# A merge of two instruction chains with its time slots halved, in an eight-core attention and gated-layer kernel

## The reference

```python
q  = apply_rope((x @ Wq + bq).reshape(B, T, 16, 64))
kv = ((x @ Wdown + bdown) @ Wup + bup).reshape(B, T, 16, 128)
k, v = split(kv); k = apply_rope(k)
att = softmax(einsum('bthd,btgd->bthg', q, k) / sqrt(64))   # heads against heads, per token
out = einsum('bthg,btgd->bthd', att, v).reshape(B, T, 1024) @ Wout + bout
x = layernorm(x + out)
x = layernorm(x + (silu(x @ wg.T) * (x @ wu.T)) @ wd.T)     # hidden 3072, integer weights / 127
```

## Time and profile before

| what | value |
|---|---|
| two timed runs | 3500.82 and 3587.18 us, median 3544.0 |
| the profiled execution's own time | 3500.25 us |
| its span on the slowest core | 3498.3 us |
| spans of the eight cores | 3476.4 to 3498.3 us |
| busy on that core: TensorE, VectorE, ScalarE, GpSimd | 2680.8, 1668.9, 803.4, 292.4 us |
| main part, tile 0 | 345 to 687 us from the span's start |
| tiles 1 to 7 | 687 to 3240 us |
| the last gated layer alone | 3240 us to the end |

### The profile page before, as it was taken

How to read it: one execution, slowest core, us unless ns; L and a number is a source line. 1 busy time by engine, 2 the same in 40 slices (tenths; PEclk the granted TensorE clock), 3 DMA queues, 4 the chain that set the end, 5 groups by cost and what they waited for, 6 DMA issues and landing times.

```text
span 3498.3 us, 41206 instructions; the slowest of 8 cores (3476.4 to 3498.3 us)
## 1 busy us (share of the span) xinstructions
PE 2680.8 (77%) x12416; PEld 1057.4 (30%) x12416; DVE 1668.9 (48%) x2454; ACT 803.4 (23%) x1361; POOL 292.4 (8%) x540
## 2 busy tenths in 40 slices
PE   0000686789888999799979998998889888988566
PEld 0000212233333333333333333333333333333222
DVE  2221355455546545474637454655565546554312
ACT  0000310142115130513042303330243124221101
POOL 0111000001100110011001100010001100110110
PEclk9999956599999999999999999999999999999778
DMA  6887200212332232323141223223322322231222
GB/s 192 244 243 206 56 1 25 42 48 62 97 73 82 61 86 77 92 63 89 61 112 52 73 82 100 64 61 94 89 77 61 100 64 82 64 97 55 93 78 82
DMA packets 108701, 303.92 MB, mean 87 GB/s; under 512 B 16192, under 2 KB 24768, under 8 KB 108496
## 3 DMA queue, kind: packets, MB, share of 16 engines
q1 hardware_dynamic: 61520, 169.14, 17.2%
q0 software_dynamic: 46976, 132.15, 13.0%
HBM read 269.77 MB, written 39.85 MB: 89 GB/s over the span
## 4 chain that ended last, share of the span: by engine, by line
PE 61%; DMA 11%; DVE 8%; issue 6%; ACT 4%; DVEq 0%; ACTq 0%; POOLq 0%; POOL 0%; SPq 0%
PE P L448 10%; PE P L762 9%; PE P L395 9%; PE P L405 8%; PE P L778 8%; PE P L671 6%; DMA wgb<-wg_s 3%; DMA wub<-wu_s 3%; DVE p_sb L725 3%; PE P L344 2%; PE P L816 2%; DMA wqb<-wq_s 2%; DMA wob<-wout_s 2%; PE P L585 2%; PE P L613 2%
## 5 line engine op out<-in xcount | busy, mean ns | idle before, releaser
L725 DVE TENSOR_TENSOR p_sb<-P,vdup_all 128x512 bf16<-128x512 f32 x1024 | 696.2, 689 | 428.5 <-PE P L778 298.7
L395 PE MATMUL P<-x_bf,wgb 128*128 128x512 bf16 x1536 | 526.1, 404 | 103.1 <-DMA wub<-wu_s 82.5
L405 PE MATMUL P<-x_bf,wub 128*128 128x512 bf16 x1536 | 494.8, 396 | 32.6 <-DVE h_sb L421 32.6
L778 PE MATMUL P<-p_sb,id_sb 128*128 128x256 bf16 x2048 | 484.5, 292 | 24.7 <-DVE p_sb L725 17.8
L448 PE MATMUL P<-h_sb,wdb 128*128 128x512 bf16 x1536 | 487.3, 385 | 14.8 <-DVE r_bf L457 13.6
L762 PE MATMUL P<-e_sb,selz_sb 16*128 16x512 bf16 x1024 | 411.9, 412 | 55.4 <-DVE p_sb L725 32.3
L646 DVE TENSOR_TENSOR hadb<-q_sb,krep 128x2048 bf16<-128x2048 bf16 x256 | 309.6, 1223 | 294.5 <-PE P L671 200.6
L671 PE MATMUL P<-hadb,selred_sb 128*16 128x256 bf16 x2048 | 326.1, 275 | 35.3 <-ACT e_sb L658 14.6
L311 PE MATMUL P<-x_bf,wd_sb 128*128 128x512 bf16 x128 | 37.8, 448 | 352.8 <-DMA x_bf<-xt 352.6
L421 DVE TENSOR_TENSOR h_sb<-s_sil,P 128x512 bf16<-128x512 bf16 x192 | 130.7, 681 | 339.3 <-PE P L405 283.2
L816 PE MATMUL P<-avn,wob 128*128 128x256 bf16 x1024 | 242.9, 285 | 51.1 <-DMA wob<-wout_s 38.8
(11 more groups left out here) (69 smaller groups left out, 1927.2 us busy)
## 6 DMA issues: line engine op xcount, KB each, us to landing
wdb<-wdn_s SPq DMA_DIRECT2D x64, 768.0 KB, 4.4
wgb<-wg_s POOLq DMA_DIRECT2D x192, 256.0 KB, 3.0
wub<-wu_s POOLq DMA_DIRECT2D x192, 256.0 KB, 3.0
wob<-wout_s SPq DMA_DIRECT2D x128, 256.0 KB, 3.1
wqb<-wq_s SPq DMA_DIRECT2D x64, 256.0 KB, 3.0
yt<-x2b SPq DMA_DIRECT2D x64, 256.0 KB, 2.2
stg<-wg SPq DMA_DIRECT2D x24, 512.0 KB, 5.3
stg<-wu SPq DMA_DIRECT2D x24, 512.0 KB, 5.2
```

Source lines behind the costliest of these rows:

```text
L395: e.matmul(o, l, r, start=st, stop=sp)),
L405: e.matmul(o, l, r, start=st, stop=sp)),
L725: add('V', (lambda e, o=o, a=a, b=b: e.tensor_mul(o, a, b)), waits=w, inc=s_v, d=640)
L778: e.matmul(o, id_sb[:, :], r, start=st, stop=sp)),
```

## The change

In the scheduler's key the slot of the earliest start becomes 200 ns instead of 400:

```diff
-                key = (round(es / 400.0), -CP[id(nd)], es)
+                key = (round(es / 200.0), -CP[id(nd)], es)
```

## The result

| | before | after |
|---|---|---|
| median of timed runs | 3505.6 us (14) | 3523.2 us (15) |
| lowest | 3498.2 | 3509.3 |
| profiled execution | 3500.25 | 3513.57 |
| its span | 3498.3 | 3511.6 |

The ratio of after to before is 1.0053, with a 95% interval of 1.0035 to 1.0071: slower by 12 to 25 us, 18.6 in the middle, and well inside 2%. The direction was as predicted and the time lies inside the range; the size was not as predicted, 5.5 us forecast.

What follows compares the result with a forecast made beforehand. Prediction: TensorE, busy 2680.8 of 3498.3 us, sets the pace in some stretches, attention's own chain in others. Second Silu 5.1 plus first h 0.4 gave +5.5 us on the profiled 3500.25, so 3506; range 3482 to 3550.

Steps and rivals of the forecast that it cites:

- The second Silu: Score stage, tiles 2 to 7: Silu between two table loads (the sandwich, 3.2 us) delays head 4 and product 6, +0.85 us each.
- The first h: Score stage, tiles 2, 3, 6 and 7: its product moves ahead of the 14 head products, +0.4 us in all.
- Hidden: Rival, 20%: ScalarE reaches the second Silu early or the products have slack, so no cost: 3500 us.
- all exposed: Rival, 14%: the sandwich delays every later score head by its full 3.2 us per tile: 3521 us.
- The burst that goes: Score stage: eight up matmuls no longer precede the last heads; priced 0, at best −11 us.
- What TensorE does meanwhile: Before the first value product: TensorE's wait for the second h grows from 2.27 to about 5 us, costing nothing.
- The value stages: Value stages: 111 insertion places instead of 114 to 119, same matmuls; priced 0, ±1 us per tile.
- The clock: Rival, 3%: after the longer wait for h TensorE stays at the half level into the value stage: 3770 us.
- Earlier weights: Rival, 3%: groups finished sooner free weight buffers sooner; all waits for gate weights and h gone would give 3430 us.
- Key and value heads, tile 1: Two steps: more gated matmuls fit among the heads, and tile 1's Silu moves into the query's evacuations; each priced 0.

## Why the prediction was right in direction and too small in size

**The second Silu** (forecast +0.85 a tile, 5.1 in all). Right. The sandwich is 3.2 us, head 4 waits 1.23 us, product 6 has a gap of 1.35. The first value product comes at +36.9 to +37.25 over tiles 2 to 7, where +36.8 was forecast. The score stages are 1.0 to 1.1 us longer in five of these tiles and 0.1 in tile 5, where four of the eight cores of before, not the one that was read, already took 1.5 us longer. That the six tiles together give 5.4 us, against 5.5 forecast with the first h, is in part luck. Moving the Silu back took 6.5 us out of the score stages (256.6 to 250.1). Hidden and all exposed are both out: it is neither +35.9 nor +39.

**The first h** (+0.4). Not separable at this size; together with the Silu the stage is within some 0.2 us of the forecast in all tiles but tile 5.

**The burst that goes** (0, at best −11). Wrong: no gain came back, as taken, but the burst had a use that the step did not ask about. It kept TensorE occupied until shortly before h was ready. With it back the first-half value stages were 13 us shorter (521.8 to 508.7).

**What TensorE does meanwhile** (0, "2 us to spare"). This is the step that failed. Its numbers were good: the wait became 4.6 to 4.8 us on the cores with all records, and the two groups behind it did end before the first value product. But it asked only whether these matmuls delay the product, not what their end releases. The third up group's end frees two weight buffers, the reload takes 3 us plus 3 us one after the other, and the fifth gate group, which stands inside the first value group, needs them. The list of waits had the row, 37.3 us for `wub` in 36 waits, and I had put these waits into stages whose order did not change; in tile 6 of before one of them, 0.48 us, already stood in the first value group.

**The value stages** (0, ±1 us). Wrong by the same cause: +13.3 us in seven first-half stages, beyond the bound of 1 us in every tile, and all of it in the first group. Worked out for tiles 2 to 7: 3.3 us more at the half level in the mean (4.3 against 1.0) at 0.43 us each are 1.4, and 0.7 for the wait, 2.1 a tile or 12.7 in six, where 12.8 were measured (both prices are taken from the same groups, so this splits the 12.8 and does not confirm it). Tile 1's first group is 3.2 us longer too, but stayed so when the weights were freed (10.7 us, median over the cores); its cause stays open. The second-half stages gained 7.7, which I had not forecast either.

**The clock** (rival, 3%). Its mechanism was there and its size was not. The lasting drop over a whole stage did not come; what came was a second short one, 4.3 us a tile in the mean. The Trainium skill, page "TensorE: Matmul & The Clock Gate", says in "HAM oscillation — how this bites in real kernels" that each idle gap lets the clock fall again, so that the loss returns with every round. I had weighed it as a drop "in a place with 2 us to spare". The traces agree for the wait for h: in all 48 places of after there is half level ahead of the first value product, 3.4 us or more. The second drop goes beyond the page's example, whose gaps are the long ones: it follows a wait of only 1.18 us, at 2601.42, and where that wait was taken away it did not come in any of 48 groups.

**Earlier weights** (rival, 3%). The sign was wrong for the pair that matters. The gate group was indeed done sooner, but the buffers are freed by the up group behind it, which was done later. Waits for `wub` went from 37.3 us in tiles 1 to 7 to 45.8, waits for h from 32.6 to 40.9 on core 4:

```profile
PE P L395 <- DMA wub<-wu_s: 45.8, 40, 3.3
PE P L405 <- DVE h_sb L421: 40.9, 14, 4.8
```

**Key and value heads, tile 1** (0). Right: 333.2 us before and after, and tile 1's score stage even 1.8 shorter.

**The numbers that came near.** The measured 3523.2 lies next to two times of the prediction that have nothing to do with it: 3522, its sum with a drain behind each table load, which the trace does not show, and 3521, with the sandwich all exposed, which would have put the first value product at +39. Nor does the place inside the range say much, since its upper end came from the spread of two timed runs.

The sum by what the runs showed: +3.6 scores, +13.3 first values, −7.7 second values, and +3.5, +4.0 and a few smaller ones elsewhere make +15.7 in the tiles, against 18.6 (12 to 25) by the ratio. The two costs and the gain of 7.7 are settled in place, the first two by experiment. No run was made for the +3.5 in the second scores, the +4.0 in the projection and the −7.7. The two runs with all up weights freed, one for each order, say a little: the projection is then 270.6 us in the new order and 272.1 in the old, so the +4.0 goes with the waits for weights; of the +3.5 1.9 is left (297.8 against 295.9), and of the −7.7 5.7 (523.4 against 529.1), so these come mostly from something else, which stays open.

## What to carry to other kernels

When a wait of the busiest engine grows in a place with time to spare, follow what the end of the waiting group releases, buffers and their reloads above all, into the next stage before pricing the wait at nothing. A filler for idle time can be worth a lot close ahead of a critical stage (13 us here); moving a wait nearer to that stage made before 0.8% slower and after another 0.4%. And look at waits between two transfers of one queue: taking one away made the kernel 2.3% faster than before, some four times what the order of the instructions had cost.

## What the runs showed that I had not expected

A wait of 0.4 to 1.5 us, in a stretch in which TensorE does short work between VectorE's products, was followed by 3 to 10 us at the half level in 31 of 48 places, when it came some 10 us after a wait of 4.6 us. Without it, after the same wait of 4.6 us, the half level came in none of 48, and so in each of three runs. The half level cost 0.43 us per microsecond there, by the estimate above, a little less than the half microsecond that a matmul of twice the length would give; that VectorE hides the rest was not shown.

Two loads of 256 KB issued together, 0.54 us apart, served the kernel clearly better than one after the other with about 3 us for each (from issue to landing the medians are 3.0 us for both before, 3.1 and 3.2 when they overlap): the waits for up weights in the last gated layer fell from 45.1 to 14.2 us.

The first-half value stages sum to the same within 1% in eight kernels (505.0 to 509.5 us), all those in which at most 16 of the 48 first groups have the half level, although the order inside the stage differs. So for this stage the slot of the merge matters through the weights and the clock. For the whole kernel 100, 200, 300 and 400 ns gave 1.0021, 1.0053, 1.0011 and 1, and between 100 and 200 the difference lies in other stages, for reasons not found.
